# Cross attention: a written order of steps over eight slots, weighing three slots behind, six buffers of exponentials, another lead

## The reference

```python
q = split_heads(layernorm(x) @ w_q.T + b_q)
k = split_heads(ctx @ w_k.T + b_k)
v = split_heads(ctx @ w_v.T + b_v)
weights = softmax(einsum('bhqd,bhkd->bhqk', q, k) / sqrt(16))
x = x + merge_heads(einsum('bhqk,bhkd->bhqd', weights, v)) @ w_o.T + b_o
```

## Time and profile before

| what | us |
|---|---|
| median of 3 runs (lowest, highest) | 4344.85 (4337.79, 4349.56) |
| the profiled execution, its time | 4319.2 |
| its span | 4317.4 |
| TensorE busy, over the span | 3977.4 (92%) |
| VectorE busy | 3008.9 (70%) |
| ScalarE busy | 2808.3 (65%) |
| POOL busy | 1810.4 (42%) |
| first Cross stage, first max to last scores | 40.0 to 980.2 |
| second Cross stage, first max to last scores | 2924.2 to 3862.3 |

### The profile page before, as it was taken

How to read it: one execution, slowest core, us unless ns; L and a number is a source line. 1 busy time by engine, 2 the same in 40 slices (tenths; PEclk the granted TensorE clock), 3 DMA queues, 4 the chain that set the end, 5 groups by cost and what they waited for, 6 DMA issues and landing times. The chain is left out here.

```text
span 4317.4 us, 81181 instructions
## 1 busy us (share of the span) xinstructions
PE 3977.4 (92%) x30224; PEld 2838.1 (66%) x30224; DVE 3008.9 (70%) x6897; ACT 2808.3 (65%) x5769; POOL 1810.4 (42%) x1862
## 2 busy tenths in 40 slices
PE   5999999988979999999999999976999999976999
PEld 3555555545757888888878888864555555544877
DVE  4777777776777777667676676644777777767845
ACT  2777777777967776777777777733766777764422
POOL 3333322303557565555555555523322232202654
PEclk7999999999989999999999999997999999997999
DMA  6666656536020101011100011017666665522365
GB/s 166 124 119 112 113 113 114 103 60 219 1 77 5 35 27 35 15 37 35 34 28 21 31 35 35 16 39 160 116 114 109 119 113 114 103 39 63 95 193 187
DMA packets 208193, 353.22 MB, mean 82 GB/s; under 512 B 26927, under 2 KB 110564, under 8 KB 205745
## 3 DMA queue, kind: packets, MB, share of 16 engines
q1 hardware_dynamic: 200217, 337.64, 35.3%
q0 software_dynamic: 7584, 10.39, 0.7%
HBM read 256.70 MB, written 114.98 MB: 86 GB/s over the span
## 5 line engine op out<-in xcount | busy, mean ns | idle before, releaser
L759 DVE TENSOR_REDUCE xa_m_part<-xa_unit 128x2 f32<-128x1024 f32 x1024 | 1247.5, 1224 | 511.2 <-PE xa_unit L907 510.0
L683 ACT ACTIVATE xa_ex<-xa_unit 128x1024 f32<-128x1024 f32 x1024 | 1030.1, 1019 | 258.5 <-PE xa_unit L891 253.2
L921 PE MATMUL xa_pv<-xa_ex,xa_vs 128*17 128x256 f32 x8192 | 546.3, 383 | 7.2 <-ACT xa_ex L683 7.0
L907 PE MATMUL xa_unit<-xa_ks,xa_q_base 48*128 48x512 f32 x2048 | 436.0, 424 | 117.3 <-ACT xa_ex L683 85.9
L1068 POOL TENSOR_SCALAR lt_p<-lt_p,lt_stat 128x192 f32<-128x192 f32 x384 | 354.5, 923 | 446.5 <-DVE lt_stat L1058 446.0
L891 PEld LDWEIGHTS xa_unit<-xa_q_base,xa_ks 50*128 50x128 f32 x4096 | 311.6, 185 | 315.9 <-issue 242.6
L891 PE MATMUL xa_unit<-xa_q_base,xa_ks 50*128 50x256 f32 x4096 | 501.0, 324 | 10.6 <-DVE xa_m_part L759 6.3
L1921 PE MATMUL lt_bank<-lt_wp,lt_xt 128*128 128x512 f32 x1728 | 467.7, 413 | 12.9 <-DVE lt_xt L1749 6.2
L1078 ACT ACTIVATE lt_p<-lt_p,lt_stat 128x128 f32<-128x128 f32 (+1 forms) x768 | 321.7, 420 | 154.4 <-DVE lt_stat L1053 151.8
L1921 PEld LDWEIGHTS lt_bank<-lt_wp,lt_xt 128*128 128x128 f32 x1728 | 316.7, 193 | 78.6 <-DVE lt_xt L1749 9.5
L618 POOL TENSOR_SCALAR xa_m_neg<-xa_m_blk 128x8 f32<-128x8 f32 x128 | 29.7, 232 | 777.0 <-DVE xa_m_blk L770 777.0
(11 more groups left out here) (334 smaller groups left out, 7908.1 us busy)
## 6 DMA issues: line engine op xcount, KB each, us to landing
xa_ks<-keys SPq DMA_DIRECT2D x372, 256.0 KB, 8.6
keys<-xa_kp SPq DMA_DIRECT2D x128, 512.0 KB, 3.3
xa_cx<-in_ctx_t SPq DMA_DIRECT2D x64, 512.0 KB, 6.0
lt_u<-in_lt_wqkv SPq DMA_DIRECT2D x54, 256.0 KB, 3.5
places<-in_moe_blank SPq DMA_DIRECT2D x47, 258.0 KB, 8.7
moe_xs<-places SPq DMA_DIRECT2D x47, 258.0 KB, 3.1
lt_w<-in_lt_w SPq DMA_DIRECT2D x6, 1408.0 KB, 6.0
xa_q_base<-xa_m_rows SPq DMA_DIRECT2D x512, 2.0 KB
```

The costliest lines, as they stand in the source:

```text
L683: act.activation(x.ex[:, n % x.NE, :, :], x.place_of[step][:, :, :].rearrange("p o (j s) -> p (o j) s", j=2), ACT.Exp).then_inc(*x.ex_done ...
L759: dve.tensor_reduce(x.m_part[:, i % 2, qt, 2 * pair:2 * pair + 2, ch:ch + 1], x.place_of[step][:, :, :], AX.X, ALU.max).then_inc(*x.dve_ou ...
L907: mm = pe.matmul(bank[:, odd, :], x.q_base[rows, pair, b * S + qt * P:b * S + (qt + 1) * P], x.ks[unit % x.NU][rows, pair % 4, ch * 512:(c ...
L921: mm = pe.matmul(x.pv[32 * j:32 * j + x.VW, 0:S], x.vs[:, i % x.NV, kt, 4 * g + j, :], x.ex[:, n % x.NE, 2 * (j % 2) + j // 2, :], start=( ...
```

## The change

`steps` no longer goes by two slots with a side step. A table ORDER of 32 tokens is walked once for each quad: W weigh, G max_rows of the next quad and gather of the one before the last, M max, S scores, X an output step or a query, K stack_k, J a job, C a part of combine. W runs BEHIND = 3 slots behind, the exponentials have NE = 6 buffers in place of 4. M runs LEAD = 17 ahead. The keys of unit 1 and the values of item 0 stand before the first M; the first two keys of item 1 stand in the lead; queries of batch b + 1 are computed in quads 7 and 9 of batch b. What follows a value or a query job (split, ctx, stack_q) has moved to `follow`, unchanged. The instructions of each step are the same as before.

```diff
@@ -269,8 +269,12 @@
     NU = 3
     NV = 2
     UNITS = 3
-    NE = 4
-    LEAD = 18
+    NE = 6
+    LEAD, ROWS_AT = 17, 14
+    AHEAD = (14, 15)
+    OUT_AT, QUERY_AT = (2, 3), (7, 9)
+    ORDER = ("W G M S M X W W S M C K J M S M J S M W W S C S M W W W S M S C").split()
+    BEHIND = 3
 
     def __init__(self, c, name, ctx_t, wq, wk, wv, wo, bq, bk, bv, bo, kscratch, load=None):
         super().__init__(c)
@@ -340,13 +344,21 @@
 
     def filling(self):
 
-
         values = lambda i: [("value", i, t) for t in range(self.KT // 2)]
-        queries = lambda b: [("query", b, mt) for mt in range(2)]
-        first = values(0)
-        out = self.keys(0, 1) + first[0:2] + queries(1) + first[2:4] + queries(2) + queries(3)
+        out = []
         for i in range(1, self.ITEMS):
             out += self.keys(i, 0) + self.keys(i, 1) + values(i)
+        return out
+
+    def follow(self, step):
+
+        out = [step]
+        if step[0] == "value" and step[2] % 2 == 1:
+            m = 2 * (step[1] + 1) + step[2] // 2
+            out += [("split", m)] if m < 2 * self.ITEMS else []
+            out += [("ctx", m + 2)] if m + 2 < 2 * self.ITEMS else []
+        if step[0] == "query" and step[2] == 1:
+            out.append(("stack_q", step[1]))
         return out
 
     def steps(self):
@@ -360,50 +372,66 @@
             out += keys[0:1] + [("split", 1), ("norm",)] + keys[1:2]
             out += queries[0:1] + [("stack_k", 0)] + queries[1:] + [("stack_q", 0), ("rest_k",)]
         out += [("ctx", 2), ("ctx", 3), ("late",)]
-        total = self.SLOTS * self.ITEMS
-        batch = self.SLOTS * self.NKB
+        for step in self.keys(0, 1) + [("value", 0, t) for t in range(self.KT // 2)]:
+            out += self.follow(step)
+            if step == ("key", 0, 1, 1):
+                out.append(("stack_k", 1))
+        total, quads = self.SLOTS * self.ITEMS, 4 * self.ITEMS
+        per_batch = 4 * self.NKB
         jobs = self.filling()
-        outputs = [(batch * (b + 1) + at, (kind, b)) for b in range(B)
-                   for at, kind in ((18, "turn_out"), (22, "project_out"))]
-        for t in range(-self.LEAD, total + 24, 2):
-            top = t + self.LEAD
-            quad, at = divmod(t, 8)
-            side = []
-            if at == 0 and 0 <= quad + 1 < 4 * self.ITEMS:
-                side.append(("max_rows", quad + 1))
-            if at == 0 and 0 <= quad - 2 < 4 * self.ITEMS:
-                side.append(("gather", quad - 2))
-            if not side and outputs and outputs[0][0] <= t:
-                side.append(outputs.pop(0)[1])
-            while len(side) < (2 if t < 0 else 1) and jobs and self.may_fill(jobs[0], t):
-                side.append(jobs.pop(0))
-            for odd in range(2):
-                if 0 <= t + odd < total:
-                    out.append(("scores", t + odd))
-                if top < total:
-                    out.append(("max", top + odd))
-                if odd == 0:
-                    out += [("weigh", n) for n in (t - 2, t - 1) if 0 <= n < total]
-            if top < total and top % 8 == 6:
-                out.append(("place_max", top // 8))
-            for step in side:
-                out.append(step)
-                if step[0] == "value" and step[2] % 2 == 1:
-                    m = 2 * (step[1] + 1) + step[2] // 2
-                    out += [("split", m)] if m < 2 * self.ITEMS else []
-                    out += [("ctx", m + 2)] if m + 2 < 2 * self.ITEMS else []
-                if step[0] == "query" and step[2] == 1:
-                    out.append(("stack_q", step[1]))
-            unit, at_u = divmod(t + 32, 16)
-            if at_u == 0 and 2 <= unit < 2 * self.ITEMS:
-                out.append(("stack_k", unit))
-            if t == 2 - self.LEAD:
-                out.append(("stack_k", 1))
-            if quad >= 2 and at >= 2:
-                b, kb = divmod((quad - 2) // 4, self.NKB)
-                if kb == self.NKB - 1 and b < B:
-                    out.append(("combine", b, (quad - 2) % 4, at // 2 - 1))
-        assert not jobs and not outputs
+        extra = {}
+        for b in range(B):
+            for at, kind in zip(self.OUT_AT, ("turn_out", "project_out")):
+                extra[per_batch * (b + 1) + at] = kind, b
+            if b + 1 < B:
+                for mt, at in enumerate(self.QUERY_AT):
+                    extra[per_batch * b + at] = "query", b + 1, mt
+        top = 0
+
+        def maximum():
+            steps = [("max", top)]
+            return steps + [("place_max", top // 8)] if top % 8 == 7 else steps
+
+        while top < self.LEAD:
+            out += maximum()
+            top += 1
+            if top == self.ROWS_AT:
+                out.append(("max_rows", 0))
+            if top in self.AHEAD:
+                out += self.follow(jobs.pop(0))
+        for quad in range(quads + 4):
+            scores, weighs, parts = 8 * quad, 8 * quad - self.BEHIND, 0
+            b, kb = divmod((quad - 2) // 4, self.NKB)
+            summing = quad >= 2 and kb == self.NKB - 1 and b < B
+            for token in self.ORDER:
+                if token == "M" and top < total:
+                    out += maximum()
+                    top += 1
+                elif token == "S":
+                    if scores < total:
+                        out.append(("scores", scores))
+                    scores += 1
+                elif token == "W":
+                    if 0 <= weighs < total:
+                        out.append(("weigh", weighs))
+                    weighs += 1
+                elif token == "G":
+                    if quad + 1 < quads:
+                        out.append(("max_rows", quad + 1))
+                    if 0 <= quad - 2 < quads:
+                        out.append(("gather", quad - 2))
+                elif token == "K" and quad % 2 == 0 and quad // 2 + 2 < 2 * self.ITEMS:
+                    unit = quad // 2 + 2
+                    assert all(k in out for k in self.keys(unit // 2, unit % 2))
+                    out.append(("stack_k", unit))
+                elif token == "J" and jobs and self.may_fill(jobs[0], scores):
+                    out += self.follow(jobs.pop(0))
+                elif token == "X" and quad in extra:
+                    out += self.follow(extra.pop(quad))
+                elif token == "C" and summing:
+                    out.append(("combine", b, (quad - 2) % 4, parts))
+                    parts += 1
+        assert not jobs and not extra and top == total
         return out
 
     def may_fill(self, job, t):
```

## The result

| | us (lowest, highest) |
|---|---|
| before, in the same measurement | 4345.12 (4337.79, 4349.56), 4 runs |
| changed | 4168.75 (4167.47, 4172.3), 4 runs |
| ratio | 0.9597, 95% [0.9583, 0.9612] |
| profiled execution of the changed kernel | 4167.85, span 4166.0 |

A forecast was written before the change was run, and what follows sets the result against it. TensorE was taken as nearest the bound (busy 94%), lengthened by tile crossings and waits on PSUM units. Loops 131 us plus leads 61 make 192 less: 4344.85 to 4153 us, with 4108 to 4205 holding 8 in 10.

The forecast's parts named there:

- The quad: Cross loop, eight slots from one max_rows to the next: TensorE's summed step durations give 12.8 us, against 13.93 before.
- M S M with its wait: First group of a quad: 0.90 us, or 1.08 because the second M waits for ScalarE to free its PSUM unit.
- W to r is a crossing: Quad's end, weigh to max_rows: charged 0.10 us as a tiling-mode change; if none, the result would be 13 us earlier.
- The rest of the loop: Each Cross loop: 59 quads with jobs, five without, six queries and three batches' output sum to 821.3 us, against 886.8.
- The lead: First max to first scores, each Cross stage: first scores at 62 us, not 93.4; 31 and 30 us less, together 61.
- Then VectorE is the bound: In the lead, VectorE's reductions at 1.13 us each set the pace; reduction 16 ends at 58.9, first scores at 62.
- the sign set for a wrong lead: Profile sign: a first scores after 75 us would show the forecast wrong in the lead.
- The slack of max_rows: Quad's end: r may start at 12.4 us and is due at 12.7 to 12.8, leaving 0.3 to 0.4.
- Rival (1): Block maxima come late from POOL, r stalls the whole quad, and the kernel gets slower: 4435 us; chance 0.04.
- each microsecond costs 128 us: In rival (1), the price of each microsecond by which block maxima are late beyond the slack of max_rows.
- the last S of a quad would stand too close: With four exponential buffers, a quad's last S would come too near the weighing four slots back; costed at nothing.
- Rival (2): Waits on ScalarE move and don't go: the loops give 70 us, not 131, total 4214 us; chance 0.10.

The follow-up runs named there:

- lead16: The changed kernel with M running 16 slots ahead, not 17; 1.0323 times the kernel before.
- ne4: The changed kernel with four buffers of exponentials again, not six; 0.9604 of the kernel before.
- the three sets: Follow-up runs of four kernels each, each set on one chip; the kernel before took 4318.67, 4353.92 and 4350.26 us in them.
- lead18: The changed kernel with M running 18 slots ahead, not 17; 0.9792 of the kernel before.

## Why the prediction was right, step by step

**The quad.** Forecast 12.8, measured 12.65. Term by term (forecast, measured): r g 0.53, 0.53; M S M with its wait 1.08, 0.97; W W 0.99, 0.99; S M 0.67, 0.66; J 1.59, 1.59; M S M 0.90, 0.91; W W W 1.43, 1.42; S M S 0.90, 0.91; last W 0.54, 0.55. The forecast's terms add up to 12.78; of the 0.13 that they are over, 0.11 is in the first M S M: the second M lost 0.07 to the step behind it (0.39 against 0.32), not 0.08 and 0.11 more. M first after a full-height step, which had no row, takes 0.34, as assumed.

**W to r is a crossing.** From the last W to r 0.55 to 0.56 pass, from W to W 0.44: 0.12, where 0.10 was charged, and as much as from a last W to S (0.99 - 0.44 = 0.55), which is a crossing for certain. The Trainium skill's "TensorEngine Tiling (Array Packing)", section Key Properties, says that changing the tiling mode, and not just the tile, drains TensorE; the trace agrees.

**The rest of the loop** came out at 819.1 and 818.4 against 821.3, and that this is so near is in part luck: the terms miss in both directions. The 59 quads with jobs are 8.9 us less (12.65 each, not 12.8). The quad with a query is 1.07 longer, not 0.8: its four matmuls take 1.06 from the first to the next step, 0.26 each, twice what one of a value job takes. Outputs add 1.09 and 1.93, 3.0 a batch, not 1.6. Together these are 5.9 more. Quads of a batch's last block last 12.86 to 12.90, and with the first quad (13.3) and one at 139.47 (13.40) that is 4.7 more, costed at nothing. The last five quads, without jobs, take 52.6 us and not 56.5, 3.9 less, though two of them run partly at a granted clock of 0.50 to 0.58.

**The lead is the term that was mis-sized.** Forecast were 31 + 30 = 61 us, measured 18.7 + 18.7 = 37.4. The step that failed is "Then VectorE is the bound". The 16 reductions end at 63.23, not 58.9: the first starts 0.8 late, VectorE idles 0.6 us at an M that waits for keys of unit 0, and 1.3 and 1.0 behind the two key jobs, the first of which takes 2.91 us at 1.2 GHz. But most, 9 of the 13.5 us, is the fetch of unit 1's keys, which the prediction named on SP's queue without asking when it lands: it is issued at 57.4 and holds the 17th M until 72.67, 10.7 us. From that M to the first scores 2.8 us pass, where 3.1 were counted behind the 16th reduction. The rows of max_rows 0, which were to land at about 60.5, are issued only at 61.08. First scores at 75.5 is also just past the sign set for a wrong lead, 75.

**The slack of max_rows** was forecast at 0.3 to 0.4 us. A block's last M starts at 384.63 and POOL's third operation ends 2.74 later, as in the earlier trace rows; r starts at 387.83 (timeline of POOL):

```profile
386.58 0.23 POOL L646 TENSOR_SCALAR xa_m_neg<-xa_m_blk 128x8 f32<-128x8 f32 x1 [1.34 <-DVE xa_m_blk L798]
...
387.16 0.21 POOL L653 TENSOR_TENSOR xa_m_cols<-xa_m_neg,xa_m_cols 128x8 f32<-128x8 f32 x1
```

0.46 us are left. Rival (1) did not come, but lead16 shows its mechanism is real, and that its price was too low: "each microsecond costs 128 us" came out at 318/1.70 = 187 by the medians. The 128 for the waits was right (2 x 106.2/1.70 = 125); what the term lacked is that stalls bring the granted clock down behind them.

**Six buffers.** The sentence that with four "the last S of a quad would stand too close" is wrong, as ne4 shows. It was costed at nothing either way, so it moved no number.

**Rival (2)**, waits on ScalarE that move, is out: M's idle time before exponentials is 0.3 us over the first loop.

**The base.** The profiled execution lay 0.6% under the median. It has the short form of the experts stage (4314.4 - 3967.3 = 347.1 us), a part that no edit touches, so counting differences from the profile and taking them off the median was right. That it ran on another chip than the median's runs is likely by the three sets, but not on record. Against the 192: the loops gave 4.6 more, the leads 23.6 less, and 3.5 lie between the stages, 176.5 in all, beside the 176.4 of the medians.

## What to carry to other kernels

Where steps take a few PSUM buffers in turn, walk the order with the readers' end times and put the long steps (jobs, groups of products) where a buffer is still being read; a change of tile costs 0.1 us each way here, a buffer asked for too soon 0.8 to 0.9 us. When waits on compute are taken out of a start-up, price each transfer that it needs by when it lands with the queues full, not by when it is issued. A slack of 0.46 us held here, with the join in its chain at its short 0.17 us (the median); look where such a short VectorE step falls beside a long one of POOL, as in lead18. Write down what it costs when missed (the waits, and TensorE's clock behind them), and try both neighbours of the constant that sets it.
